# Decoder kernel: column groups at the start of the first stage, cross-attention weights loaded and split in the last turns of the self-attention

## What is computed

```python
# sublayer 1, self-attention: 16 heads of 128, 4 groups of key and value heads
q = (x @ Wq).reshape(b, n, H, HD).transpose(0, 2, 1, 3)
k = (x @ Wk).reshape(b, m, HKV, HD).transpose(0, 2, 1, 3)
v = (x @ Wv).reshape(b, m, HKV, HD).transpose(0, 2, 1, 3)
q = q * cq + rotate_half(q) * cq          # the same table for both terms
k = k * ck + rotate_half(k) * ck
...
x = _layernorm(x + softmax(q k^T * scale) v @ Wo)
# sublayer 2, attention over the context and the own row block
q = rms_norm(x @ wq, q_norm_w); k = rms_norm(x @ wk, k_norm_w)
k_ctx = rms_norm(ctx @ wk_ctx, k_norm_w); v_ctx = ctx @ wv_ctx; v = x @ wv
q = q * cos + rotate_half(q) * sin; k = k * cos + rotate_half(k) * sin
scores = q [k_ctx, k]^T * scale + mask
x = _layernorm(x + softmax(scores) [v_ctx, v] @ wo)
```

## Time and profile before

| | |
|---|---|
| median of 3 runs | 2896.91 us (2895.69 to 2898.89) |
| the profiled execution: time | 2890.31 us |
| the profiled execution: span | 2888.5 us |
| mean granted TensorE clock | 0.965 |
| TensorE busy | 2667.9 us (92%) |
| VectorE busy | 1879.2 us (65%) |
| ScalarE busy | 1311.8 us (45%) |
| GpSimd busy | 1248.2 us (43%) |

### The profile page before, as it was taken

The page is one execution under the profiler, slowest core; times in us unless marked ns, Lnnn a source line. Parts: engine busy times, 40 slices in busy tenths (PEclk is TensorE's granted clock), DMA queues, the critical chain, the costliest instruction groups (busy, mean ns, idle before and its releaser), DMA issues. The chain is left out here.

```text
span 2888.5 us, 65059 instructions
## 1 busy us (share of the span) xinstructions
PE 2667.9 (92%) x23764; PEld 2306.1 (80%) x23764; DVE 1879.2 (65%) x4014; ACT 1311.8 (45%) x3138; POOL 1248.2 (43%) x1605
## 2 busy tenths in 40 slices
PE   6999999994999999999999889996999999699995
PEld 5999999994888888888888768885777777477774
DVE  5555556554777777777777654444777777366766
ACT  2222222223666666666666533332433334266665
POOL 3111121122576777777676501113455454334444
PEclk9999999997999999999999989997999999799998
DMA  4000000002000000000000020001000000000001
GB/s 144 8 7 7 4 7 7 7 0 99 6 4 5 4 4 5 4 5 4 5 4 5 0 75 0 0 0 33 9 8 11 7 11 0 26 27 26 29 12 59
DMA packets 42507, 49.16 MB, mean 17 GB/s; under 512 B 4032, under 2 KB 33600, under 8 KB 41920
## 3 DMA queue, kind: packets, MB, share of 16 engines
q1 hardware_dynamic: 42432, 48.16, 5.0%
HBM read 35.56 MB, written 4.19 MB: 14 GB/s over the span
## 5 line engine op out<-in xcount | busy, mean ns | idle before, releaser
L528 POOL TENSOR_TENSOR a_probs<-a_probs,a_rs 128x512 f32<-128x512 f32 x64 | 66.8, 1044 | 482.4 <-DVE a_rs L421 482.4
L1109 POOL TENSOR_TENSOR b_rows<-b_rows,b_swapped 128x512 f32<-128x512 f32 x160 | 204.4, 1286 | 56.0 <-DVE b_swapped L895 55.9
L1050 ACT ACTIVATE b_probs<-bank,b_shift,b_q_scale 128x128 f32<-128x128 f32 x512 | 228.2, 461 | 0.7
L1156 POOL TENSOR_TENSOR b_probs<-b_probs,b_rs 128x512 f32<-128x512 f32 x128 | 133.2, 1040 | 137.0 <-DVE b_rs L947 133.8
L2593 ACT ACTIVATE d_probs<-d_probs 128x512 f32<-128x512 f32 x128 | 78.9, 630 | 242.7 <-DVE d_probs L2492 240.8
L485 ACT COPY a_pT<-bank 128x512 f32<-128x512 f32 x64 | 37.5, 586 | 326.3 <-PE bank L300 326.3
L46 PE MATMUL bank<-a_xT,a_wq 128*128 128x256 f32 x512 | 150.3, 293 | 26.4 <-DVE a_xT L388 26.4
L1119 POOL TENSOR_TENSOR b_rms<-b_rms,sh_minus_half 128x8 f32<-128x8 f32 (+1 forms) x128 | 169.6, 1325 | 10.7
L903 DVE TENSOR_REDUCE b_ss<-b_squares 128x4 f32<-128x512 f32 x192 | 125.2, 680 | 73.7 <-ACT b_squares L1025 73.7
L46 PE MATMUL bank<-b_wo,b_oT 128*128 128x256 f32 x512 | 150.8, 295 | 1.4 <-DVE b_oT L869 1.4
L426 DVE TENSOR_TENSOR a_oT<-bank,a_oT 128x512 fp32r<-128x512 f32 x128 | 82.5, 686 | 103.2 <-ACT a_oT L490 103.2
(11 more groups left out here) (350 smaller groups left out, 8923.8 us busy)
## 6 DMA issues: line engine op xcount, KB each, us to landing
a_xT_in<-in_xT SPq DMA_DIRECT2D x16, 256.0 KB, 2.7
sh_x<-in_x SPq DMA_DIRECT2D x1, 4096.0 KB, 24.9
b_ctx_in<-in_ctxT SPq DMA_DIRECT2D x32, 128.0 KB, 2.0
d_x_in<-sh_x SPq DMA_DIRECT2D x16, 256.0 KB, 2.3
e_x_in<-sh_x SPq DMA_DIRECT2D x16, 256.0 KB, 2.3
e_cT<-in_ctxT SPq DMA_DIRECT2D x32, 128.0 KB, 2.5
out<-sh_x SPq DMA_DIRECT2D x16, 256.0 KB, 2.1
a_qT<-in_L_attn_Wq SPq DMA_DIRECT2D x1, 2048.0 KB, 8.5
```

The costliest lines, as they stand in the source:

```text
L1050: op = act.activation(probs[:, g % 2, keys], bS[:, keys], ACT.Exp, bias=shift[:, g % 2, a:a + 1], scale=q_scale[:, g, a // 2, a % 2:a % 2 ...
L1109: pool.tensor_tensor(rows[:, unit, :], rows[:, unit, :], swapped[:, half, :], ALU.add).then_inc(added[unit], 1)
L1156: pool.tensor_tensor(pr, pr, rs[:, g % 2, :].unsqueeze(2).to_broadcast([128, R, 128]), ALU.mult).then_inc(probs_ready[g], 1)
```

## The change

In the first stage the query weights are loaded, folded and split in four groups of 512 columns, one for each group of heads, and the projection of a group in turn 0 waits for its own piece. The order on VectorE in turn 0 is written out: folds, low parts and evictions alternate. The high part of the output weights is made by ScalarE, GpSimd keeps the subtraction. The semaphores of the loop are raised by GpSimd and ScalarE. The second turn's rows are requested ahead of x.

`EarlyWeights` holds weight tensors that both stages use. Query and key weights of the cross-attention are loaded behind x, its context key weights after the last value projection. Six pieces of them are split in the last two turns of the self-attention, into the tensors of its own query, key and value weights. 61 semaphores of the second stage are allocated ahead and raised by the first stage's DMA queue. The second stage begins with turn 0's copies; it loads tables first, then the two value weights, which are split within turn 0 ahead of the value projection. An outer block around both stages is closed with a clearing of its semaphores and a barrier.

```diff
+        wq, wk, wv, wo = sh.early.wq, sh.early.wk, sh.early.wv, sh.early.wo
...
+        with nc.sbuf_tensor("a_next_context", [128, C, G * HD], F32) as stage:
+            next_context = stage[:, :, :]
...
+        raw = [qT[:, g, :, :, :].rearrange("p b r q -> p (b r q)").rearrange("p (c n) -> p c n", c=C) for g in range(G)]
+        raw.append(kT[:, :, :].rearrange("p g n -> p (g n)").rearrange("p (c n) -> p c n", c=C))
+        folded = [folded_q[:, g] for g in range(G)] + [probs[:, :, :]]
...
+        K, V, O = G, G + 1, G + 2
+        columns = [slice(g * R * HD, (g + 1) * R * HD) for g in range(G)]
+        pieces = [(wq[:, 0, :, columns[g]], wq[:, 1, :, columns[g]], folded[g]) for g in range(G)]
+        pieces += to_split(wk, folded[K], 1) + to_split(wv, full_v, 1) + to_split(wo, full_o, 1)
...
-            for s in looped:
-                sp.sem_inc(s, 1)
-            sp.dma_start(raw_k, t["L0_attn_Wk"].rearrange("(c p) n -> p c n", p=128)).then_inc(w_loaded[0], 16)
+            def load_columns(g):
+                sp.dma_start(raw[g], t["L0_attn_Wq"].rearrange("(c p) n -> p c n", p=128)[:, :, columns[g]]).then_inc(w_loaded[g], 16)
+            load_columns(0)
             sp.dma_start(xT_in[:, :, :], t["xT"][0]).then_inc(xT_loaded, 16)
-            sp.dma_start(raw_q, t["L0_attn_Wq"].rearrange("(c p) n -> p c n", p=128)).then_inc(w_loaded[1], 16)
+            load_columns(1)
             sp.dma_start(cos[:, :], t["cosT"]).then_inc(tables_loaded, 16)
             sp.dma_start(sh.ident[:, :], t["ident"]).then_inc(tables_loaded, 16)
-            sp.dma_start(full_v, t["L0_attn_Wv"].rearrange("(c p) n -> p c n", p=128)).then_inc(w_loaded[2], 16)
-            sp.dma_start(full_o, t["L0_attn_Wo"].rearrange("(h p) n -> p h n", p=128)).then_inc(w_loaded[3], 16)
+            load_columns(2)
+            load_columns(3)
+            sp.dma_start(raw[K], t["L0_attn_Wk"].rearrange("(c p) n -> p c n", p=128)).then_inc(w_loaded[K], 16)
+            sp.dma_start(full_v, t["L0_attn_Wv"].rearrange("(c p) n -> p c n", p=128)).then_inc(w_loaded[V], 16)
+            sp.dma_start(full_o, t["L0_attn_Wo"].rearrange("(h p) n -> p h n", p=128)).then_inc(w_loaded[O], 16)
+            def load_turn(i, source):
+                sp.wait_ge(x_low, nth(i - 1, 1, 1))
+                sp.dma_start(xT_in[:, :, :], source).then_inc(xT_loaded, 16)
+            load_turn(1, t["xT"][1])
...
-            with sp.Fori(1, n_turns) as i:
-                sp.wait_ge(x_low, nth(i - 1, 1, 1))
-                sp.dma_start(xT_in[:, :, :], t["xT"][bass.ds(i, 1), :, :, :].rearrange("a p c n -> (a p) c n")).then_inc(xT_loaded, 16)
+            sh.early.load(sp, t)
+            for s in sh.cross.values():
+                sp.sem_inc(s, 1)
+            with sp.Fori(2, n_turns) as i:
+                load_turn(i, t["xT"][bass.ds(i, 1), :, :, :].rearrange("a p c n -> (a p) c n"))
+            sp.wait_ge(proj_ready, nth(n_turns - 1, 12, 12))
+            sh.early.load_context(sp, t)
         @block.tensor
         def _(pe):
+            def needs(i, n):
+                if type(i) is int and i == 0:
+                    pe.wait_ge(w_ready, n + 1)
             def q_proj(i, g):
...
                     last.then_inc(proj_ready, 1)
             def k_proj(i):
+                needs(i, K)
                 for u in range(2):
                     pe.wait_ge(proj_dve, nth(i, 10, 7 + u))
...
             def weigh_values(i, g):
+                if type(i) is int and i == 0:
+                    pe.wait_ge(wo_step, 1)
                 pe.wait_ge(pT_taken, nth(i, G, g + 1))
...
-            pe.wait_ge(w_ready, len(pieces) - 1)
             pe.wait_ge(zeroed, 1)
             turn(0, None, None)
-            pe.wait_ge(wo_step, 2)
...
+            def fold(n):
+                dve.wait_ge(w_loaded[n], 16)
+                halves = raw[n].rearrange("p c (h a e) -> p c h a e", a=2, e=HD // 2)
+                out = folded[n].rearrange("p c (h a e) -> p c h a e", a=2, e=HD // 2)
+                dve.tensor_tensor(out[:, :, :, 0, :], halves[:, :, :, 0, :], halves[:, :, :, 1, :], ALU.subtract).then_inc(w_folded, 1)
+                dve.tensor_tensor(out[:, :, :, 1, :], halves[:, :, :, 1, :], halves[:, :, :, 0, :], ALU.add).then_inc(w_folded, 1)
+            def low_w(n):
+                split_low(dve, pieces[n], n, w_high, w_ready)
...
                 if older is not None:
                     low_o(older, G - 1)
+                    if before is None:
+                        ahead.low(dve, G + 1)
...
                         total(before, g)
+                        if now is None:
+                            ahead.low(dve, g)
...
                 if before is not None:
                     low_o(before, G - 2)
+                    if now is None:
+                        ahead.low(dve, G)
                 if now is not None:
                     take_k(now, 0)
                     take_k(now, 1)
...
+            fold(0)
+            low_x(0)
+            fold(1)
+            low_w(0)
+            fold(2)
+            low_w(1)
+            dve.wait_ge(tables_loaded, 32)
+            take_q(0, None, 0)
+            fold(3)
+            low_w(2)
+            take_q(0, None, 1)
+            fold(K)
+            low_w(3)
+            take_q(0, None, 2)
+            low_w(K)
+            take_q(0, None, 3)
+            low_w(V)
+            take_k(0, 0)
+            take_k(0, 1)
             turn(1, 0, None)
...
-                    for g in range(2, G):
-                        take_pT(before, g - 1)
-                        take_o(before, g - 2)
+                    for g in range(G):
+                        if g >= 1:
+                            take_pT(before, g - 1)
+                        if g >= 2:
+                            take_o(before, g - 2)
                         exponent(before, g)
+                        if now is None:
+                            ahead.high(act, g)
                     take_pT(before, G - 1)
                     take_o(before, G - 2)
+                    if now is None:
+                        ahead.high(act, G)
+                        ahead.high(act, G + 1)
                     take_o(before, G - 1)
                 if now is not None:
...
                     high_x(following)
+            for s in looped[1::2]:
+                act.sem_inc(s, 1)
             high_x(0)
+            for n in range(len(pieces)):
+                high_w(n)
             turn(0, None, 1)
...
             pool.memset(sh.minus_half[:, :], -0.5).then_inc(zeroed, 1)
             pool.wait_ge(zeroed, 1)
-            split_on_pool(pool, pieces[-1], w_loaded[3], wo_step)
+            high, low, full = pieces[O]
+            pool.wait_ge(w_high, O + 1)
+            pool.tensor_tensor(low, full, high.bitcast(F32), ALU.subtract).then_inc(wo_step, 1)
             pool.wait_ge(x_loaded, 16)
             def turn(now, before):
...
         def sem(name):
+            if name in sh.cross:
+                return sh.cross[name]
             s = nc.alloc_semaphore("b_" + name)
             looped.append(s)
             return s
...
+        wq, wk, wkc, wo = sh.early.wq, sh.early.wk, sh.early.wv, sh.early.wo
...
             sp.dma_start(ctx_in[:, :, :], t["ctxT"][0]).then_inc(ctx_loaded, 16)
-            for n, name in enumerate(("wk_ctx", "wv_ctx", "wk", "wv")):
-                sp.dma_start(pieces[n][2], t["L0_xattn_" + name].rearrange("(c p) n -> p c n", p=128)).then_inc(w_loaded[n], 16)
-            for c in range(C):
-                sp.dma_start(full_q[:, c], t["L0_xattn_wq"][c * 128:(c + 1) * 128, :]).then_inc(w_loaded[4 + c], 16)
             for n, name in enumerate(("q_norm_w", "k_norm_w")):
                 sp.dma_start(norm_w[:, n, :], t["L0_xattn_" + name].rearrange("(a n) -> a n", a=1).to_broadcast([128, HD])).then_inc(tables_loaded, 16)
             sp.dma_start(cos, t["cos_rows"]).then_inc(tables_loaded, 16)
             sp.dma_start(sin, t["sin_rows"]).then_inc(tables_loaded, 16)
-            sp.dma_start(probs[:, 0, :], t["causal"]).then_inc(tables_loaded, 16)
-            sp.dma_start(full_o, t["L0_xattn_wo"].rearrange("(h p) n -> p h n", p=128)).then_inc(w_loaded[4 + C], 16)
+            for n, name in enumerate(("wv_ctx", "wv")):
+                sp.dma_start(pieces[n][2], t["L0_xattn_" + name].rearrange("(c p) n -> p c n", p=128)).then_inc(w_loaded[n], 16)
+            sp.dma_start(probs[:, 0, :], t["causal"]).then_inc(causal_loaded, 16)
             for s in looped:
                 sp.sem_inc(s, 1)
+            sp.dma_start(full_o, t["L0_xattn_wo"].rearrange("(h p) n -> p h n", p=128)).then_inc(w_loaded[2], 16)
             with sp.Fori(1, sh.turns) as i:
                 sp.wait_ge(ctx_low, this(i - 1))
                 sp.dma_start(ctx_in[:, :, :], t["ctxT"][bass.ds(i, 1)].rearrange("a p c n -> (a p) c n")).then_inc(ctx_loaded, 16)
...
+                if first(i):
+                    pe.wait_ge(w_ready, 2)
                 project(i, V, xT, wv)
```

(68 more changed lines are left out.)

104 lines of the change are left out of this document (43 added, 61 removed).

## The result

The changed kernel takes 2881.38 us (median of 5 runs, 2879.72 to 2885.1) against 2895.69 for the kernel before (5 runs): ratio 0.9953, 95% interval 0.9942 to 0.9965, 14.3 us faster. A second comparison of the same two kernels gave 2885.15 against 2896.65: ratio 0.9965 (0.9953 to 0.9978), 11.5 us. I had forecast 26.1 us and 2870.8, and the upper end of my range was 2881.0. So the sign was right, and about half of the gain is missing.

What follows compares the result with a forecast made beforehand. TensorE, always busy in both long loops, bounds the kernel; only its standstills at start and border could give. -13.8 - 15.6 + 2.6 + 0.7 = -26.1 us, from 2896.9 to 2870.8 us; range 2864 to 2881.

Steps and rivals of the forecast that it cites:

- rival B: Start: GpSimd's 9.04 us subtraction holds up VectorE's subtraction of the next activations by 4 us, giving 2875; chance 0.06.
- Cost of all this: 0: Start: output weights' cast on ScalarE, GpSimd's subtraction, later x load and moved semaphore increments all stay in time, costing 0.
- -13.8: Start of the self-attention: less work ahead of the first matmul brings the next activations' low part 13.8 us earlier.
- The last two turns, 0: End of the self-attention: six casts and six subtractions fit into idle time and cost 0; 7.3 us if none were covered.
- rival C: Self-attention's last turns: the splits' 7.3 us of VectorE time are exposed and reach the output chain, giving 2878; chance 0.07.
- The border, -15.6: Between the two stages: with loads and splits gone, the first context projection starts at about 684.4 instead of 700.04, 15.6 us earlier.
- The extra closing: After the cross-attention: one more clearing of semaphores and one more barrier cost 0.7 us, between 0 and 1.5.
- Turn 0, +2.6: Cross-attention's turn 0: value weights' splits between the squares and sums make what follows 2.6 us later; free 0, serial 4.4.
- A: Start: TensorE stays at the lower clock level through turn 0, losing 9.4 us, giving 2880; chance 0.12.
- D: Border: the new stage's first instructions or the tables bind, only half of 15.6 us is won, giving 2878.6; chance 0.07.
- E: Both long loops: moved code slows instruction fetch, 0.6 us per turn cancels the gain, 1 us gives 2915; chance 0.03.
- value projections done near 31: Sign for the start: turn 0's value projections end at 31.5 us, before at about 45.2.

Runs made afterwards that it cites:

- experiment 1: The kernel before with one wait added: GpSimd's cast of the output weights starts only after VectorE's last split of the start; 2894.66 us in one execution.
- experiment 2: The changed kernel with one wait added: GpSimd's subtraction for the output weights starts only after VectorE's subtraction for the value weights; 2873.13 us, ratio 0.9931.
- experiment 3: The changed kernel with the output weights' subtraction moved from GpSimd to VectorE, behind the evictions of the keys; 2873.59 us, ratio 0.9922.
- experiment 9: The changed kernel with the cross-attention's turn 0 splits placed ahead of the first query group's square and sum; 2878.96 us, ratio 0.9942.

## Why the prediction was wrong

**The step that failed** is the sentence that dismissed rival B: "GpSimd's cast at 18.68 ran over VectorE's two subtractions of 2048 columns at 19.07, which took 4.49 together ... the trace should show a delay there; it shows none". The delay was there, on the other engine. VectorE's row was continuous, and it was the cast that stood still: 3.60 us of work in a record of 10.08 (experiment 1). I checked whether the instruction that I was worried about (VectorE's) had been slow, and not whether its partner had been. ScalarE's cast of as many elements at 3.61, in the same group, was the hint; I used both numbers as prices, and asked of neither why they differed by a factor of three.

By the same step **"Cost of all this: 0"** for GpSimd's subtraction was wrong. Rival B found the victim too late as well: it put the only overlap at the low part of turn 1's rows, 4 us (2875), and that is what experiment 2 measured, once the earlier meeting was taken away. In the changed kernel the subtraction came at 27.04, the forecast was 26.7, and VectorE's last weight split started at 27.11. Had GpSimd's subtraction started 0.1 us later it would, by what the last two turns show, have been the one held; no run tested that. What was missing was to lay GpSimd's whole interval over every two-operand instruction of VectorE. The hold took 8.65 us, and after TensorE's pause of 8.52 us its value projections ran at the lower level, 2.4 us more (12 matmuls at 0.43 apart and not at 0.23). That is 11.0 of the 11.7 us between -13.8 and -2.1. The rest was there ahead of the hold: the query evictions ended 0.6 us later than I had followed them. Without the hold the sequence was right: the low part of turn 1's rows came up at 32.93 in experiment 2, forecast 32.7, and in experiment 3, behind 4.42 us more of VectorE's work, at 33.42, a gain of 13.1.

**The last two turns, 0** (rival C at 7.3 exposed). The work itself was covered, as I had said. What was not: each split stands right after the reciprocal that releases GpSimd, so all four normalisations were held by 0.9 to 1.0. That costs 1.5 us, again the rule of rival B; a gap of VectorE's was free of VectorE's work but not of GpSimd's. The rest, 1.7 in one trace and 3.3 in the other, is TensorE at its lower level. It occurs without the splits too (experiment 1), and what sets it off in these turns stays open.

**The border, -15.6:** -14.3, right in mechanism: the first context projection waited for the increment behind eight issues, as named. I had it 5.4 us after the last write, it came 6.72 after. One of the eight issues took 1.64 us and not 0.52, and the step from the last write to the first issue 0.5 more (1.52 against 1.02), which I had not counted here. **The extra closing** after the cross-attention, +0.7, was 0.4 (2.04 against 1.64 us from GpSimd's last write to the next DMA).

**Turn 0, +2.6:** measured +3.5 and +2.9. The way was right: x's value projection starts 2.7 us later after the first context projection than before (19.69 against 17.01), and experiment 9 brings 2.3 to 2.9 back by moving just these splits. The other 0.9 in the first trace is TensorE's: it was granted 1.00 from 706 to 709 us and 0.52 from 709 to 712.5, the value projection took 2.09 us instead of 1.69 and the turning of four blocks behind it 1.06 instead of 0.60. The second trace has no such fall there. A hold is in both traces, of GpSimd's reciprocal root (2.49 instead of 1.65 beside VectorE's splits), but it is off the chain: GpSimd's next instruction after it, at 709.45, came only after 2.28 us of waiting for VectorE.

**Rivals A, D, E.** A did not happen as written: the first 28 matmuls were 0.21 us apart, until 16.1 us, near the 5.1 us for a group that I had put in, those of the other queries and the keys 0.12, and only the value projections fell back to the lower level, after a pause that was GpSimd's doing. D and E did not happen; the loops' rate is unchanged. Of the unchanged later stages, the one behind the cross-attention is 1.4 to 2.1 us longer in eight traces of after and its variants (303.1 to 303.9, against 301.5 to 301.9 in three of before's), and 302.0 to 302.4 in the other three; its cause stays open.

**What would have shown it:** "value projections done near 31" and "GpSimd's first normalisation near 36.5" were the right signs. They came at 43.2 and at 48.21. In kernel 3, without the hold, the projections were done at 31.2 and the normalisation ran at 37.23.
